# Row sums turned earlier in the step, and one chunk of the transposed adjacency from a block-wise load and VectorE

## The reference, cut to what matters

```
h  = relu(layernorm(x))                              # per node, over 128 features
HW[r] = h @ W[r, :128] + c[r]                        # r = 0..6, c[r] = W_edges[r] @ W[r, 128:]
A  = [adj, adj, shifted, adj^T, adj^T, shifted^T, eye]
out = max over r of (A[r] @ HW[r]) + b
return x + out
```

## Time and profile before

| | us |
|---|---|
| median of 3 runs | 223.4 (222.56 to 223.49) |
| the profiled execution's own time | 223.7 |
| its span in the trace | 221.7 |
| PE busy | 211.5 (95%) |
| ACT busy | 186.0 (84%) |
| DVE busy | 179.2 (81%) |
| POOL busy | 163.8 (74%) |
| DMA queue of SP, share of the 16 DMA engines | 70.3% |

### The profile page before, as it was taken

The page is one execution under the profiler, slowest core; times in us unless marked ns, Lnnn a source line. Parts: engine busy times, 40 slices in busy tenths (PEclk is TensorE's granted clock), DMA queues, the critical chain, the costliest instruction groups (busy, mean ns, idle before and its releaser), DMA issues.

```text
span 221.7 us, 4960 instructions
## 1 busy us (share of the span) xinstructions
PE 211.5 (95%) x1069; PEld 174.5 (79%) x1069; DVE 179.2 (81%) x388; ACT 186.0 (84%) x468; POOL 163.8 (74%) x179
## 2 busy tenths in 40 slices
PE   7898999999999999999999999999999999999980
PEld 5777678887888888888888888888888888887760
DVE  3795799796989879797887969887887969777683
ACT  3767999998998989898898989899898989887640
POOL 1370499979596996969697896969699696969241
PEclk9999999999999999999999999999999999999997
DMA  5928976959596986768596877758597776236725
GB/s 178 302 91 184 243 199 171 263 113 252 135 248 143 245 180 157 231 158 215 122 254 145 198 206 155 235 136 218 131 230 190 165 222 146 43 53 143 158 37 89
DMA packets 91152, 38.71 MB, mean 175 GB/s; under 512 B 71575, under 2 KB 80903, under 8 KB 91143
## 3 DMA queue, kind: packets, MB, share of 16 engines
q1 hardware_dynamic: 90055, 38.48, 70.3%
q10 hardware_dynamic: 1088, 0.13, 0.4%
HBM read 34.33 MB, written 4.26 MB: 174 GB/s over the span
## 4 chain that ended last, share of the span: by engine, by line
PE 85%; DVE 6%; ACT 2%; DMA 2%; issue 2%; SPq 0%; DVEq 0%; ACTq 0%
PE at_ps L745 11%; PE rel_ps L765 11%; PE rel_ps L767 11%; PE rel_ps L766 11%; PE bwd_ps L765 6%; PE bwd_ps L767 6%; PE bwd_ps L766 6%; PE fwd_ps L765 6%; PE fwd_ps L767 6%; PE fwd_ps L766 6%; PE turn_ps L753 3%; DMA a_sb<-in_adj 2%; DVE h_lo L692 1%; DVE best L595 1%; PE rel_ps L762 1%
## 5 line engine op out<-in xcount | busy, mean ns | idle before, releaser
L304 POOL TENSOR_TENSOR a_lo<-a_sb,a_hi 128x512 fp32r<-128x512 f32 x62 | 79.1, 1298 | 37.8 <-ACT a_hi L386 37.8
L595 DVE TENSOR_TENSOR best<-rel_ps,best 128x512 f32<-128x512 f32 x62 | 42.6, 687 | 13.7 <-PE rel_ps L767 13.6
L566 DVE TENSOR_TENSOR at_lo<-at_ps,at_hi 128x512 fp32r<-128x512 f32 x62 | 41.2, 685 | 8.2 <-ACT at_hi L394 7.6
L434 ACT ACTIVATE rel_ps<-sum_all,c_col 128x512 f32<-128x512 f32 (+1 forms) x63 | 41.8, 679 | 4.5 <-DVE best L595 2.9
L386 ACT ACTIVATE a_hi<-a_sb 128x512 fp32r<-128x512 f32 x64 | 39.4, 617 | 3.8 <-DMA a_sb<-in_adj 3.8
L394 ACT ACTIVATE at_hi<-at_ps 128x512 fp32r<-128x512 f32 x62 | 36.3, 590 | 6.5 <-PE at_ps L745 6.3
L745 PEld LDWEIGHTS at_ps<-ident,a_sb 128*128 128x128 f32 x240 | 28.1, 141 | 4.2
L745 PE MATMUL at_ps<-ident,a_sb 128*128 128x128 f32 x240 | 31.2, 272 | 0.0
L592 DVE SCALAR_TENSOR_TENSOR best<-rel_ps,c_col,best 128x512 f32<-128x512 f32 x32 | 23.9, 747 | 6.9 <-PE rel_ps L767 5.8
L319 POOL TENSOR_TENSOR xb_sb<-xp_sb,bias_sb 128x512 f32<-128x512 f32 x16 | 22.7, 1421 | 5.9 <-DMA xp_sb<-in_x 5.9
L765 PE MATMUL bwd_ps<-a_hi,h_hi 128*128 128x512 f32 x64 | 27.0, 421 | 0.0
(11 more groups left out here) (103 smaller groups left out, 438.9 us busy)
## 6 DMA issues: line engine op xcount, KB each, us to landing
a_sb<-in_adj SPq DMA_DIRECT2D x64, 256.0 KB, 3.3
sum_all<-sums_dram SPq DMA_DIRECT2D x16, 512.0 KB, 4.1
x_sb<-in_x SPq DMA_DIRECT2D x16, 256.0 KB, 3.7
xp_sb<-in_x SPq DMA_DIRECT2D x64, 64.0 KB, 3.6
out<-o_sb SPq DMA_DIRECT2D x60, 64.0 KB, 2.0
w_sb<-in_L_gnn_W SPq DMA_DIRECT2D x1, 448.0 KB, 6.0
sums_dram<-sum_rows SPq DMA_DIRECT2D x16, 4.0 KB
bias_sb<-in_L_gnn_b SPq DMA_DIRECT2D x4, 64.0 KB, 2.2
```

What stands on the lines that cost most here:

```text
L304: pool.tensor_tensor(a_lo[q][:, j, :], a_sb[q][:, j, :], a_hi[q][:, j, :].bitcast(fp32), ALU.subtract).then_inc(a_lo_ready[j], 1)
L434: act.activation(to[:, cols], sum_all[q][:, 0 if r in FWD else 1, cols], ACT.Copy, scale=c_col[:, r:r + 1]).then_inc(after_it, 1)
L566: dve.tensor_tensor(at_lo[q][:, i, :], at_bank(b, i)[:], at_hi[q][:, i, :].bitcast(fp32), ALU.subtract).then_inc(at_lo_ready[i], 1)
L595: dve.tensor_tensor(best[q][:], held[:], best[q][:], ALU.max).then_inc(joined[r], 1)
```

## The change

Four things are changed together.

1. **Sums.** `turn_sums` moves from behind `turn_h` to behind `fwd(k, q, 1)`, into bank `at_ps[0]` instead of `rel_ps[1]`. It then waits for `split_at` of chunk 2, whose bank it takes over. `take_sums` on ScalarE moves to behind `join_first`. Batches 0 and 1 keep the old place.
2. **Chunk 3 of the transpose.** From batch 1 on TensorE no longer turns it. The last 128 columns of the adjacency are loaded a second time, block-wise (`load_a_blocks`, four DMAs of 64 KB), and VectorE turns them with one block transpose (`turn_a_blocks`), called behind `round_h`.
3. **SP's order.** In a step of the loop SP now: stores the sums of batch b; loads the adjacency of batch b + 2, in two DMAs of 512 KB instead of four of 256 KB; spreads the sums; stores the output of batch b - 2; loads x of batch b + 2; loads x of batch b by blocks; loads the blocks of batch b + 2.
4. **Waits** follow: `turn_a` of chunk 0 waits for `take_sums`, chunk 1 for the split of chunk 1 of the batch before; `eye` of EYE[2] no longer waits for the sums except in batches 0 and 1.

```diff
@@ SP
             def reload_a(k, q):
                 b = 2 * k + q
-                sp.wait_ge(a_turned[C - 1], b + 1)
-                for j in range(C):
-                    sp.wait_ge(a_lo_ready[j], b + 1)
-                    load_a(k + 1, q, j)
+                sp.wait_ge(a_turned[C - 2], b + 1)
+                if is_batch(b, 0):
+                    sp.wait_ge(first_turned, 1)
+                for first in range(0, C, 2):
+                    sp.wait_ge(a_lo_ready[first], b + 1)
+                    sp.wait_ge(a_lo_ready[first + 1], b + 1)
+                    sp.dma_start(a_sb[q][:, first:first + 2, :],
+                                 adj[2 * k + 2 + q, first * P:(first + 2) * P, :].rearrange("(j p) m -> p j m", p=P)
+                                 ).then_inc(a_loaded[q][first + 1], 16)
+
+            def load_a_blocks(k, q):
+                b = 2 * k + q
+                wait(sp, a_turned[C - 1], b - 1)
+                load_by_blocks(a_blocks, adj[b, :, (C - 1) * P:], a_blocks_loaded)
...
             def step(k, q, more, stored=True):
-                sums_first = is_batch(2 * k + q, 0) or is_batch(2 * k + q, B - 1)
-                if sums_first:
-                    spread_sums(k, q)
-                if more:
+                if is_batch(2 * k + q, 1):
+                    reload_x(k, q)
+                    reload_a(k, q)
+                store_sums(k, q)
+                if is_batch(2 * k + q, 0):
+                    load_by_blocks(bias_sb, bias, bias_loaded)
+                elif more and not is_batch(2 * k + q, 1):
+                    reload_a(k, q)
+                spread_sums(k, q)
+                if is_batch(2 * k + q, 0):
                     reload_x(k, q)
                     reload_a(k, q)
                 if stored:
                     store(k - 1, q)
-                if not sums_first:
-                    spread_sums(k, q)
+                if more and not is_batch(2 * k + q, 0) and not is_batch(2 * k + q, 1):
+                    reload_x(k, q)
                 load_xp(k, q)
+                if more:
+                    load_a_blocks(k + 1, q)
@@ ScalarE
-                if not left:
-                    take_sums(k, q, at_ps[0])
                 join_first(k, q)
+                if not second:
+                    take_sums(k, q)
@@ VectorE
+            def turn_a_blocks(k, q):
+                b = 2 * k + q
+                dve.wait_ge(a_blocks_loaded, G * 16 * b)
+                if not is_batch(b, 1):
+                    dve.wait_ge(at_lo_ready[C - 1], b)
+                dve.transpose(at_last[:], a_blocks[:]).then_inc(a_turned[C - 1], 1)
...
                     round_h(*ahead)
+                    turn_a_blocks(*ahead)
                 join(*prev, FWD[1])
@@ TensorE, step
                 fwd(k, q, 1)
-                if not left:
-                    pe.wait_ge(at_lo_ready[2], B)
-                    turn_sums(k, q, at_ps[0])
+                if not is_batch(b, 1):
+                    turn_sums(k, q)
                 eye(k, q, EYE[1])
...
                     turn_h(*ahead)
+                if is_batch(b, 1):
                     pe.wait_ge(joined[EYE[1]], b + 1)
-                    turn_sums(k, q)
+                    turn_sums(k, q, rel_ps[1])
...
                 if left:
                     turn_a(*ahead, 2)
-                    turn_a(*ahead, 3)
@@ TensorE, turn_sums
+                if not is_batch(b, 1):
+                    pe.wait_ge(at_lo_ready[1 if is_batch(b, 0) else 2], b + 1)
```

More of the change, by code:

```diff
@@ L108, in gnn_layer, with is_batch, at_from @@
         sums_dram = [nc.dram_tensor(f"sums_dram{q}", [S, P], fp32, kind="Internal").ap() for q in range(2)]
-        def at_bank(b, i):
+        def is_batch(b, n):
+            return isinstance(b, int) and b == n
+        def at_from(b, i):
+            if i == C - 1 and not is_batch(b, 0):
+                return at_last
             return rel_ps[i] if isinstance(b, int) and b == 0 and i < 2 else at_ps[i % 2]
@@ L390, in round_at @@
                 b = 2 * k + q
-                act.wait_ge(a_turned[i], b + 1)
+                if is_batch(b, 0) and i == C - 1:
+                    act.wait_ge(first_turned, 1)
+                else:
+                    act.wait_ge(a_turned[i], b if i == C - 1 else b + 1)
                 wait(act, fwd_done, b - 1)
                 wait(act, sums_turned, b - 1)
-                act.activation(at_hi[q][:, i, :], at_bank(b, i)[:], ACT.Copy,
+                act.activation(at_hi[q][:, i, :], at_from(b, i)[:], ACT.Copy,
                                accum_out=sums[q][:, 1, i:i + 1]).then_inc(at_hi_ready[i], 1)
@@ L490, in step @@
                     round_at(*ahead, 0)
-                    take_sums(k, q)
+                    if second:
+                        take_sums(k, q, rel_ps[1])
                 else:
@@ L736, in turn_a @@
                 if i == 0:
-                    for j in range(C):
+                    for j in range(C) if isinstance(k, int) and k == 0 else (1, 3):
                         pe.wait_ge(a_loaded[q][j], 16 * (k + 1))
-                if i >= 2:
-                    pe.wait_ge(at_lo_ready[i - 2], b + 1)
+                if i == 2:
+                    pe.wait_ge(at_lo_ready[0], b + 1)
+                elif i == 0:
+                    pe.wait_ge(at_lo_ready[2], b)
+                    if not is_batch(b, 2):
+                        pe.wait_ge(sum_rows_ready, b)
                 else:
-                    pe.wait_ge(at_lo_ready[i + 2], b)
+                    pe.wait_ge(at_lo_ready[C - 1 if is_batch(b, 1) else 1], b)
                 for j in range(C):
-                    last = pe.transpose(at_bank(b, i)[:, j * P:(j + 1) * P], a_sb[q][:, j, i * P:(i + 1) * P], ident[:])
+                    last = pe.transpose(at_from(b, i)[:, j * P:(j + 1) * P], a_sb[q][:, j, i * P:(i + 1) * P], ident[:])
                 last.then_inc(a_turned[i], 1)
@@ L811, in eye @@
                 else:
-                    pe.wait_ge(sum_rows_ready, b + 1)
-                    if not (isinstance(b, int) and b == 0):
+                    if is_batch(b, 0) or is_batch(b, 1):
+                        pe.wait_ge(sum_rows_ready, b + 1)
+                    if not is_batch(b, 0):
                         pe.wait_ge(joined[EYE[1]], b + 1)
@@ L840, in first_step @@
                 bwd(0, 0, 3)
-                turn_sums(0, 0)
+                turn_sums(0, 0, rel_ps[1])
                 turn_a(*ahead, 0)
```

31 lines of the change are left out of this document (14 added, 17 removed).

## The result

The changed kernel takes 293.7 us (289.75 to 294.82, 4 runs) against 223.4: ratio 1.305 [1.298, 1.312]. The ratio is taken over the two of the four runs that lie within 1.5% of the fastest (291.4 us in the mean), and the profile is of a run of 294.3 us, just outside. The forecast was 262, in a range of 236 to 280: the right side and the right wait, but some 30 us too little.

The account below looks back on a forecast made before the run. PE was taken to bound the kernel (95% busy, step 12.71 us). From 223.7 us, minus 1.3 for three shortened steps, plus 39.5 for twelve steps stretched to 16.0 us, gave 261.9, so 262 us; range 236 to 280.

Parts of the forecast that it names:

- The late x load: SP's queue, steps 2 to 13: DVE's moments wait 3 to 5 us for x, adding 39.5 us in all.
- The step's length: Chain through x, sums and stores in the loop: a step lasts 16.0 us instead of 12.71; this case's chance 0.60.
- SP's issues: SP's queue ahead of x: the output's store begins at t + 5.5, takes 2.0 us, so x is issued at t + 7.5.
- the clock: Rival, PE in the loop: granted clock falls too, 1.3 to 1.4 us more per step, about 278 us; chance 0.10.
- the landing: x load behind the queue: lands 4.9 us after its issue, between 2.9 (fastest x load) and 5.5 to 5.6.
- The saved transposes: PE, 15 batches: four transposes fewer save 0.44 us each, 6.6 us; a PE-bound step would last 12.27 us.
- VectorE's added transpose: DVE: one block transpose of 0.70 us raises its work to 11.34 us of a 12.27 us step, and fits.
- The earlier sums give nothing: Sums turned earlier: no gain by themselves, since ACT waited only 0.9 us for spread sums in the whole run.

Follow-up runs that it names:

- run 1: Changed kernel with the x load moved to the head of SP's step, ahead of the sums' store: 222.66 us, ratio 0.9976 to the kernel before.
- run 3: Kernel before with only its x load moved behind the output's store from batch 2 on: 235.6 us, ratio 1.054.
- run 4: Changed kernel with chunk 2's four transposes made seven times in the loop, keeping PE busy in its gap: 282.8 us, ratio 1.264 to the kernel before.
- run 7: Changed kernel with both adjacency DMAs moved behind the x load, x staying behind the output's stores: 246.7 us, ratio 1.107 to the kernel before.
- run 2: Changed kernel with the x load moved ahead of the output's four stores, still behind sums, adjacency and spreading: 273.9 us, ratio 1.226 to the kernel before.
- run 6: Changed kernel with the x load behind the sums' store but ahead of the adjacency: 225.9 and 229.7 us, too far apart for a ratio.
- run 8: Changed kernel with x load heading SP's step, turn_sums one relation later, ScalarE's sums copy behind its first fill: 224.6 us, ratio 1.0065 to the kernel before.
- run 10: Changed kernel with x load heading SP's step and VectorE's turn_best moved behind split_at of chunk 2: 228.2 us, ratio 1.022 to the kernel before.
- run 12: Changed kernel, x load heading SP's step, turn_sums one relation later, sums copy behind first fill, VectorE's block transpose behind join of FWD[1]: 222.5 us, ratio 0.9974.
- run 5: Kernel before with only the block-wise loads (end of SP's step) and VectorE's transpose added; sums, x, adjacency at old places: 241.2 us, ratio 1.081.

## Why the prediction was wrong

**The late x load: right.** That DVE's moments would wait on x_sb in twelve steps, and PE at the head of the next step behind them, is shown by the waits, by run 1 (all of the loss gone) and by run 3 (the same wait made in the kernel before).

**The step's length: wrong, 16.0 for 18.53.** The terms of the sum against the round shown above:

| from, to | forecast | measured |
|---|---|---|
| `eye(EYE[0])` to `turn_sums` | 1.93 | 134.67 - 132.11 = 2.56 |
| to SP's store of the sums | 0.70 | 0.74 |
| to the spreading's issue | 1.60 | 1.62 |
| to x's issue | 2.5 | 140.25 - 137.03 = 3.22 |
| to the moments | 4.95 | 145.63 - 140.25 = 5.38 |
| to the next `eye(EYE[0])` | 4.31 | 4.36 |
| sum | 15.99 | 17.88 |

The same sum in three pieces, now the mean of twelve rounds, beside the two runs that took a piece away (from the timelines of SP and DVE):

| from, to | forecast | changed | run 4 | run 7 |
|---|---|---|---|---|
| SP's store of the sums to x's issue | 4.1 | 5.09 | 5.08 | 4.42 |
| x's issue to the moments | 4.95 | 5.58 | 5.67 | 3.15 |
| the moments to the next store of the sums | 6.94 | 7.71 | 6.92 | 6.95 |
| sum | 15.99 | 18.38 | 17.67 | 14.52 |

Three terms were too small, and they close the step. (18.38 lies a little under the 18.53 above, whose window ends on other instructions.) The largest is SP's issues, 1.0 us. I priced the four stores by rows taken with little outstanding, 2.0 us; behind the adjacency they take 2.2 to 3.0. The old trace could have told: the x load of the earlier trace rows was held for 2.4 us at its issue.

```profile
24.52 2.41 SPq L199 DMA_DIRECT2D x_sb<-in_x  x1
```

The second is the clock, 0.8: in the text it was a rival of 0.10 at 1.35 us a step. It came true, and run 4, with the clock up, brings the last piece back to the forecast. The third is the landing, 0.6, where I took 4.9 against my own sum's 5.5 and the row's 5.6, "because packets overlap". It was 5.58 in the mean of the twelve late loads, 4.84 to 6.10. (The tile's median of 5.4 includes the four early loads.)

Runs 7 and 2 show the common root: the adjacency's megabyte ahead of x. It lengthens the landing, slows SP's issues, and so opens the gap in which the clock falls. Run 7 takes it away, and the clock's piece is at its forecast, SP's issues are within 0.3 us of theirs, and the landing is 1.8 below.

The Trainium skill, "DMA: Bandwidth & Descriptors", section "Queues, rings and completion order", on which the longer step was weighed (descriptors are consumed in ring order), holds here: x lands in 2.9 us with nothing of the step's big loads ahead (run 6), in 3.1 behind spreading and stores (run 7), in 5.4 behind all of it (medians of the tile).

On the clock, the skill's "TensorE: Matmul & The Clock Gate", section "HAM oscillation — how this bites in real kernels", describes a DMA wait in each round after which each round starts at half rate. The trace agrees: PE idled 2.8 to 5.8 us at the head of each of the twelve rounds, and its passes were at the slow pace from the first on in seven of them, and from a few passes later in the other five. My argument against it, that the gap would be shorter than the 3.3 us of the earlier trace rows and interrupted by `fwd`'s first passes, did not hold: in the next round of the chain above PE idled 2.81 us, until 148.76, ran `fwd`'s three passes at full pace, and the granted clock was 0.50 from 150.5 to 153 us. At the 3 us of my own 16.0 us step the fall should have been the forecast and not a rival.

**The saved transposes: right as a term, lost in the whole.** Run 1's step is 12.61 us instead of the 12.27 of PE's list; without the 0.27 us of waiting at `turn_sums` it would be 12.34, so the list is about as short as forecast. The run's 0.7 us of gain are within what a measurement can tell. I had priced VectorE's added transpose and the sums' new place at nothing because the sums of busy time fit (VectorE 137.38 of 151.34 us in that run). Fitting by the sum is not fitting in order: runs 8 and 10 each took away TensorE's wait at `turn_sums` and got a wait on ScalarE for it. Run 12 took away both, and PE waited for `split_ht` at the head of the step. Two readings are left. One is that the step is passed round between TensorE, VectorE and ScalarE. The other, which none of these runs removes, is SP's queue: it has no slack in run 1 and none in run 12, where the moments come 2.6 to 3.0 us behind x's issue and wait for x seven times (3.7 us in all, 1.8 of it at the start). A run with fewer issues on SP, or with some of them on another queue, would decide. Until then what holds the step at 12.6 us stays open.

**"The earlier sums give nothing": open for the old queue, doubtful beside the blocks.** In the old queue ScalarE waited 0.9 us for the sums; no run moved them there alone. With the blocks and the sums late, run 5 waited 25.1 us.

## What to carry to other kernels

Moving one DMA in an in-order queue moves all that stand behind it: for each, write down who reads the data, at what point of its own in-order list, and what else is queued there. Price a load by what is issued ahead of it, and not by the median of its old place: 3.7 us became 5.6 here. Price the issues the same way: they too get longer behind a full queue, and the issuing engine can run out of slack by them. And where a wait repeats in each round, don't set the falling clock aside as an independent rival: here it fell in all twelve rounds of the changed kernel.

## What the runs showed of the hardware

- The spreading (each of 128 partitions reads the same 4 KB) starts slowly: 139 to 147 GB/s for a microsecond directly behind the adjacency load, with the DMA share at 0.94 to 1.03 (run 2), and 66 to 147 GB/s from 206.0 to 207.0 us in the kernel before, with nothing big ahead, at shares of 0.50 and 0.64. There it then moved at 360 and 336 GB/s. Which DMA moved in a window is inferred from the order of issue.
- An x load that takes 0.4 us of SP's queue to issue when little is outstanding took 2.2 to 3.1 us behind 1.75 MB. Which issue is held depends on what stands ahead: with x ahead of the stores (run 2) x takes 0.37 us and the four stores 5.6 and 5.9.
- After a gap of 4.3 us PE's passes followed one another by 0.43 us from 130.69 to about 136.6, and by 0.23 from there on. The clock also fell after idle stretches of 2.8 us (changed kernel, until 148.76) and of 1.5 us (run 7, until 125.48).
